# Where attention hands over to the mLSTM stage: batch 0's queries, the gates' second half and ten units

## The reference, cut to what matters

```
x = x + attn(layernorm(x))               # causal softmax, 16 heads of 16; its output is reshaped (heads, time) before W_out
x = x + mlstm(q=layernorm(x), k=v=ctx)   # 8 heads of 32
x = x + moe(layernorm(x))                # 8 experts, top 2, 256 -> 1024 -> 256, exact gelu
# inside mlstm:
pre = 15 * tanh((concat(q, k, v) @ ifgate_w.T + b) / 15); i_pre, f_pre = first 8, last 8
lf  = cumsum(log_sigmoid(f_pre))
log_d[t, s] = lf[t] - lf[s] + i_pre[s] for s <= t;  m[t] = max_s log_d[t, s]
s_mat = (q @ k.T / sqrt(32)) * exp(log_d - m)
h = s_mat @ v / (max(|sum_s s_mat|, exp(-m)) + 5e-5);  h = h * rsqrt(mean(h*h) + 1e-6) * gain
```

## Time and profile before

| | |
|---|---|
| median of 3 runs | 1012.65 us (1009.31 to 1014.28) |
| the profiled execution | 1014.33 us, of which span 1012.5 us |
| PE / PEld busy | 88% / 66% of the span |
| DVE, ACT, POOL busy | 61%, 48%, 52% |
| longest shares of the chain that ended last | PE 57%, DVE 12%, ACT 8%, POOL 6%, issue 6%, DMA 6% |

### The profile page before, as it was taken

The page is one execution under the profiler, slowest core; times in us unless marked ns, Lnnn a source line. Parts: engine busy times, 40 slices in busy tenths (PEclk is TensorE's granted clock), DMA queues, the critical chain, the costliest instruction groups (busy, mean ns, idle before and its releaser), DMA issues.

```text
span 1012.5 us, 31650 instructions
## 1 busy us (share of the span) xinstructions
PE 890.3 (88%) x11877; PEld 664.1 (66%) x11966; DVE 621.5 (61%) x1340; ACT 483.9 (48%) x808; POOL 524.8 (52%) x660
## 2 busy tenths in 40 slices
PE   4798898989896567999899798899999999999995
PEld 3566666666664345666666487687877878787783
DVE  4766777687764345777777756655555555555552
ACT  3556666666765345564655434233333333333331
POOL 2545655655664233568788766643435343444342
PEclk8999999999997878998988879999999999999998
DMA  9112333234233444445555323343333333333222
GB/s 282 52 34 64 82 108 107 75 85 135 76 85 116 105 128 151 128 145 171 168 173 172 102 69 85 81 92 49 51 48 50 50 50 49 51 50 51 49 29 26
DMA packets 133199, 92.97 MB, mean 92 GB/s; under 512 B 75713, under 2 KB 114113, under 8 KB 132929
## 3 DMA queue, kind: packets, MB, share of 16 engines
q1 hardware_dynamic: 119760, 73.10, 26.2%
q0 software_dynamic: 13296, 17.83, 10.6%
HBM read 54.65 MB, written 37.32 MB: 91 GB/s over the span
## 4 chain that ended last, share of the span: by engine, by line
PE 57%; DVE 12%; ACT 8%; POOL 6%; issue 6%; DMA 6%; SPq 2%; POOLq 0%; DVEq 0%; ACTq 0%
PE pair L946 18%; PE pair L960 9%; PE pair L962 7%; PE pair L661 3%; PE pair L675 3%; PE pair L639 3%; POOL sm L1560 3%; DMA o_scr<-On 2%; PE pair L688 2%; DMA STG<-wup_in 2%; PE pair L817 1%; PE pair L912 1%; DMA out_d<-XB 1%; DVE SD L1140 1%; ACT xn L1313 1%
## 5 line engine op out<-in xcount | busy, mean ns | idle before, releaser
L946 PE MATMUL pair<-XTs,WU 128*128 128x128 bf16 x3408 | 287.3, 221 | 9.9 <-DVE XTs L1281 4.1
L946 PEld LDWEIGHTS pair<-XTs,WU 128*128 x3408 | 241.2, 99 | 77.6 <-issue 14.8
L1597 POOL DMA_INDIRECT out_d<-XB x71 | 115.1, 1621 | 209.3 <-DVE XB L1303 180.3
L1473 ACT ACTIVATE Hf<-pair 128x512 f32<-128x512 f32 x142 | 84.8, 597 | 227.8 <-PE pair L946 224.8
L960 PE MATMUL pair<-WD,Hh 128*128 x479 | 181.8, 380 | 0.0
L1294 DVE CAST Hh<-Hf 128x512 bf16<-128x512 f32 x142 | 63.9, 450 | 172.6 <-ACT Hf L1473 172.6
L962 PE MATMUL pair<-WD,Hl 128*128 x568 | 155.1, 273 | 5.0 <-issue 0.2
L1518 POOL TENSOR_SCALAR_AFFINE_SELECT PT<-PT 128x512 f32<-128x512 f32 (+1 forms) x96 | 74.4, 788 | 67.2 <-ACT PT L1332 60.7
L1296 DVE TENSOR_TENSOR Hl<-Hf,Hh 128x512 bf16<-128x512 f32 x142 | 99.8, 703 | 4.9
L1032 DVE TENSOR_REDUCE mxn<-pair 128x4 f32<-128x1024 f32 x64 | 75.3, 1218 | 27.4 <-PE pair L620 27.3
L1140 DVE TENSOR_TENSOR SD<-pair,SD 128x1024 f32<-128x1024 f32 x48 | 58.7, 1223 | 41.0 <-ACT SD L1415 25.5
(11 more groups left out here) (237 smaller groups left out, 1810.8 us busy)
## 6 DMA issues: line engine op xcount, KB each, us to landing
XB<-xs_scr SPq DMA_DIRECT2D x71, 130.0 KB, 2.1
STG<-wup_in SPq DMA_DIRECT2D x32, 256.0 KB, 4.8
q_scr<-SPL SPq DMA_DIRECT2D x16, 512.0 KB, 3.8
STG<-wdn_in SPq DMA_DIRECT2D x32, 256.0 KB, 2.7
o_scr<-On SPq DMA_DIRECT2D x32, 128.0 KB, 4.1
Mm<-o_scr SPq DMA_DIRECT2D x16, 256.0 KB, 3.0
CnT<-ctxt_in SPq DMA_DIRECT2D x16, 256.0 KB, 4.3
CX<-ctx_in SPq DMA_DIRECT2D x16, 256.0 KB, 3.4
```

What stands on the lines that cost most here:

```text
L946: t = e.matmul(upb(j, k)[:, 128 * (fm % 4):128 * (fm % 4) + 128], WU[:, bass.ds(reg[j] * 4096 + off, 128)], XTs[:, r, hx, dk, :], start=n ...
L1473: e.activation(Hf[:, r, hs], upb(j, k), ACT.Gelu).then_inc(gel.sem, 1)
L1597: e.indirect_dma_start(out=out, out_offset=bass.IndirectOffsetOnAxis(ap=XS[:, i % NX, 256:257].bitcast(I32), axis=0), in_=Yf[:, i % NY, :] ...
```

## The change

- `attn_steps`: batch 0's `queries` take the place of Gs and GE at iteration 16 behind PV 14; Gs of q = 0 goes to the end of iteration 15, ahead of AX; GE goes behind the last iteration, ahead of PV 15; MG 17 (the gate sums of batch 12) is added behind PV 15; `contexts` are steps of their own, for batch 0 behind A4 15 and for batch 1 at the end.
- In MG, the maxima's transposes come ahead of the gate sums.
- ScalarE copies the input gates, times 15, from PSUM into `gg_` before Exp; VectorE adds the running sum to it there; the bank is free once Exp has read it. For q = 0 the splitting uses a free part of Q for its remainder, and no longer waits for GE's transposes.
- `rest` spreads over ten units (0,0) to (4,2) other than before: some units take more, GA 13 to 15, XQ 14 and 15 and the gates come later, and A6c 14 sooner.
- The query tiles are set to zero one by one, the first in iteration 15; the order of tiles in SBUF changes so that this part of WD lies over tiles free by then.

```diff
@@ attn_steps
         if i == B:
-            yield "Gs", 0, 0
-            yield "GE", 0, 0
+            yield "queries", 0, 0
             yield "Gp", 0, 0
             yield "Go", 0, 0
             yield "decays", 0, 0
...
         if ok(i - 2):
             yield "A4", i - 2, 0
+        if i == B - 1:
+            yield "Gs", 0, 0
         if ok(i + 2) or ok(i - 4):
             yield "AX", i, 0
...
-    yield "queries", 0, 0
+    yield "GE", 0, 0
     yield "PV", B - 1, 0
+    yield "MG", B + 1, 0
     yield "A4", B - 1, 0
+    yield "contexts", 0, 0
     yield "decays", 1, 0
     yield "queries", 1, 0
+    yield "contexts", 1, 0
@@ mlstm_steps
-    rest = {(0, 0): (("GA", z - 3), ("A6s", z - 2), ("Mm", z), ("X1", z - 1), ("A6n", z - 2), ("A6c", z - 2)),
-            (0, 1): (("A6s", z - 1), ("XQ", z - 2), ("A6n", z - 1)),
-            (0, 2): (("A6c", z - 1), ("X1", z), ("A6s", z), ("GA", z - 2)),
-            (1, 0): (("XQ", z - 1), ("A6n", z)), (1, 1): (("A6c", z), ("GA", z - 1)), (1, 2): (("XQ", z),),
-            (2, 0): (("GA", z), ("Gt", 1)), (2, 1): (("GT", 1),), (2, 2): (("Gs", 1),),
-            (3, 0): (("GE", 1),), (3, 1): (("Gp", 1),), (3, 2): (("Go", 1),)}
+    rest = {(0, 0): (("A6s", z - 2), ("Mm", z), ("X1", z - 1), ("A6n", z - 2), ("A6c", z - 2)),
+            (0, 1): (("A6s", z - 1), ("XQ", z - 2), ("A6n", z - 1), ("A6c", z - 1)), (0, 2): (("X1", z), ("A6s", z)),
+            (1, 0): (("GA", z - 2), ("A6n", z)), (1, 1): (("XQ", z - 1), ("A6c", z)), (2, 0): (("XQ", z),), (2, 1): (("GA", z - 1),),
+            (3, 0): (("GA", z), ("Gt", 1)), (3, 1): (("GT", 1),), (3, 2): (("Gs", 1),), (4, 0): (("GE", 1),), (4, 1): (("Gp", 1),),
+            (4, 2): (("Go", 1),)}
@@ release of the pair (and of tb) by GT
-                w.wait_ge(g_dve.sem, g_dve.at("gg", b))
+                w.wait_ge(g_act.sem, g_act.at("exp", b))
@@ tensor_attn, MG: the gate sums of b - 5 now behind the transposes of Mp
@@ vector_gate_scans
-            e.scalar_tensor_tensor(gg_[:, :], ps[0:64, 0:256], 15.0, cs_, ALU.mult, ALU.add).then_inc(g_dve.sem, 1)
+            e.tensor_tensor(gg_[:, :], gg_[:, :], cs_, ALU.add).then_inc(g_dve.sem, 1)
@@ vector_gate_parts
-            w.wait_ge(g_pe.sem, g_pe.at("emT", q))
+            if q:
+                w.wait_ge(g_pe.sem, g_pe.at("emT", q))
+            rest = (gf, r1b[q])
@@ scalar_gates, GT
+                e.activation(gg_[:, :], ps[0:64, 0:256], ACT.Copy, scale=15.0)
                 e.activation(gf, ps[0:64, 256:512], ACT.Exp, scale=-15.0).then_inc(g_act.sem, 1)
@@ gpsimd_attn, GT
                     w.wait_ge(vmm.sem, vmm.at(B - 1))
+                    e.memset(QS[0][:, 0:2048].bitcast(F32), 0.0).then_inc(qb_z, 1)
...
-            for q in QS:
-                e.memset(q[:, 0:2048].bitcast(F32), 0.0).then_inc(qb_z, 1)
+            e.memset(Q1[:, 0:2048].bitcast(F32), 0.0).then_inc(qb_z, 1)
@@ tensor_mlstm S, and queries
-                    w.wait_ge(qb_z, 2)
+                    w.wait_ge(qb_z, min(b, 1) + 1)
@@ contexts
-            w.wait_ge(vmm.sem, vmm.at(B - 1))
+            w.wait_ge(t2m.sem, t2m.at(B - 1, 1))
```

More of the change, by code:

```diff
@@ L295, in build @@
         ca = ExitStack()
+        WQh = sb("WQh", [128, 2, 768], BF, ca)
+        WQl = sb("WQl", [128, 2, 768], BF, ca)
+        K = sb("K", [128, NQ, 2, 2, 256], F32, ca)
+        Q = sb("Q", [128, NQ, 2, 256], F32, ca)
+        Mp = sb("Mp", [128, 2, 2, 4, 32], BF, ca)
+        MT = sb("MT", [128, 2, 256], BF, ca)
         xTh = sb("xTh", [128, 2, 2, 256], BF, ca)
         xTl = sb("xTl", [128, 2, 2, 256], BF, ca)
-        WQh = sb("WQh", [128, 2, 768], BF, ca)
-        WQl = sb("WQl", [128, 2, 768], BF, ca)
         xn = sb("xn", [128, 2, 256], F32, ca)
-        K = sb("K", [128, NQ, 2, 2, 256], F32, ca)
-        Q = sb("Q", [128, NQ, 2, 256], F32, ca)
         sel = sb("sel", [128, 2, 128], BF, ca)
         mxn = sb("mxn", [128, 2, 2, 4, 2], F32, ca)
-        Mp = sb("Mp", [128, 2, 2, 4, 32], BF, ca)
-        MT = sb("MT", [128, 2, 256], BF, ca)
         OTs = sb("OTs", [128, 4, 256], F32, ca)
@@ L318, in build @@
         gf, cs_ = r1[:, 0, :], r1[:, 1, :]
+        r1b = (Q[0:64, (B - 3) % NQ, 0, :], cs_)
         gg_ = sb("gg_", [64, 256], F32, ca)
@@ L351, in build @@
         te8 = sb("te8", [128, 67, E], F32)[:, 0:NF, :]
-        spare = sb("spare", [128, 172], F32)
+        spare = sb("spare", [128, 168], F32)
         WD = sb("WD", [128, E * 4096], BF)
@@ L487, in high @@
             return t.bitcast(BF).rearrange("p (c h) -> p c h", h=2)[:, :, 1]
-        g_dve = sig("g_dve", [(k, q) for q in range(2) for k in ("cs", "gg", "MM", "run", "neg", "em", "pp")])
+        g_dve = sig("g_dve", [(k, q) for q in range(2) for k in ("cs", "gg", "MM", "run", "neg", *(("em", "pp") if q else ("pp", "em")))])
         g_act = sig("g_act", [(k, q) for q in range(2) for k in ("tanh", "exp", "ln", "em")])
@@ L735, in tensor_attn @@
                         t.then_inc(mpT.sem, 1)
+                    if ok(b - 5):
+                        tensor_gate_sums(e, w, b - 5, ps[:, 1, 0:32])
                 elif kind == "GT":
@@ L1077, in vector_attn @@
                 elif kind == "Gs":
-                    vector_gate_scans(e, w, b, pair_of("GT", b)[:, 0, :])
+                    vector_gate_scans(e, w, b)
                 elif kind == "GE":
@@ L1109, in vector_gate_parts @@
             w.wait_ge(g_dve.sem, g_dve.at("neg", q))
-            w.wait_ge(g_pe.sem, g_pe.at("emT", q))
+            if q:
+                w.wait_ge(g_pe.sem, g_pe.at("emT", q))
+            rest = (gf, r1b[q])
             for n in range(3):
                 for k, src in enumerate((gg_, MM)):
-                    v = src[:, :] if n == 0 else r1[:, k, :]
+                    v = src[:, :] if n == 0 else rest[k]
                     t = e.tensor_copy(pp[:, 3 * k + n, :], v)
@@ L1117, in vector_gate_parts @@
                 for k, src in enumerate((gg_, MM)):
-                    v = src[:, :] if n == 0 else r1[:, k, :]
+                    v = src[:, :] if n == 0 else rest[k]
                     if n < 2:
-                        e.tensor_tensor(r1[:, k, :], v, pp[:, 3 * k + n, :], ALU.subtract).then_inc(dvc.sem, dvc.up())
+                        e.tensor_tensor(rest[k], v, pp[:, 3 * k + n, :], ALU.subtract).then_inc(dvc.sem, dvc.up())
                 w.wait_ge(dvc.sem, dvc.n)
@@ L1153, in vector_mlstm @@
                 elif kind == "Gs":
-                    vector_gate_scans(e, w, b, tb)
+                    vector_gate_scans(e, w, b)
                 elif kind == "GE":
@@ L1671, in sync_attn @@
                     queries(e, w, b)
+                elif kind == "contexts":
                     contexts(e, w, b)
```

4 lines of the change are left out of this document (1 added, 3 removed).

## The result

Medians: 1008.45 us after the change (12 runs, 1005.76 to 1010.12), 1012.65 before (12 runs, 1009.31 to 1017.57); ratio 0.9949, 95% interval 0.9933 to 0.9965. By the ratio the change gains 5.1 us of the 12 forecast (by the medians 4.2), and its time lies 7.8 above the predicted 1000.7, at the upper end of the range of 994.5 to 1009. The profiled execution took 1006.74 us around a span of 1005.0.

What follows compares the result with a forecast made beforehand. The bound taken was the matmul engine's waits between attention's last batch and the second stage's first unit. First S 12.5 us sooner, +0.5 over ten units: 12 off 1012.65 gives 1000.7 us, range 994.5 to 1009.

Steps and rivals of the forecast that it cites:

- Step 1: ScalarE's copy of the gates, taken at 0.38 us, frees the bank so that T0 of batch 15 starts 1.8 us sooner.
- Step 2: Scans before batch 11's low half: query split ends at 323.9; no cost if it ties with T0 15, 0.5 us if late.
- Step 3: GE behind attention's T2: T0's other half 3.5 us sooner, batch 12's norm 5.9 us sooner, PV 15 at 336.1.
- Step 4: Batch 0's queries issued by 327.6 and landed by 331.1, so the 6.92 us wait ahead of the first S goes.
- The carry: From batch 5 on the order is as before, so the experts start 12 us sooner.
- the rest over ten units: New order of left-over work, batches 0 to 4: sum +1 us, bounds -5 and +8, taken as +0.5.
- The first rival: ScalarE's waits in batches 0 to 4 do not overlap: +6 in place of +0.5, 1006.2 us; chance 0.17.
- gate sums 13: They held batch 1's D unit 3.98 us for batch 15's residual; moved behind D and S: -3, bounds -4 and 0.
- The norm: Batch 15's norm, ahead of batch 14's transposes, holds ScalarE from D's exponential of unit (1,1): +2.5 us, bounds 0 and 4.
- The gates: Table loads and scans move to batch 3, gg's 2.21 us wait goes: -2; GE and splitting in batch 4: +2.
- The clock: Matmul engine longer at 1.2 GHz in the 16 batches: up to 5 us per 10 us, 1019.2 with 37; chance 0.06.
- Another transfer in the queries' place: Decays or batch 14's merged output come late, first units wait, 6.9 us of gain go: 1007.5 us; chance 0.09.

Runs made afterwards that it cites:

- copy_only: Kernel before plus only ScalarE's copy of the gates, its release and VectorE's plain add: 1020.18 us, ratio 0.9991.
- again: The changed kernel run once more, unedited, beside its variants: 1006.74 us, ratio 0.9942 to the kernel before.
- old_rest: Changed kernel with the `rest` table of the kernel before: 1000.05 us, ratio 0.9872; run once more, 0.9847.
- groups 2 to 4: Follow-up kernels in three sets, each on one chip beside the kernel before, whose medians there were 1022.91, 1019.97 and 1020.34 us.
- group 1: First set of follow-up kernels, run on one chip beside the kernel before, whose median there was 1012.66 us.
- norm_order: Changed kernel with query transposes XQ 14 put ahead of the norm of batch 15 again, in unit (1,0): 1006.36 us, ratio 0.9925.
- ge_bank: Changed kernel with the second half's GE transposes in a free part of bank 7, not waiting for hh: 1015.84 us, ratio 0.9941.
- context_first: old_rest with batch 14's context moved ahead of unit (0,2), as in the changed kernel: 1011.13 us, ratio 0.9908.
- old_rest2: old_rest once more, unedited, as the base of the last group: 1006.94 us, ratio 0.9847.
- queries_late_old_rest: old_rest with batch 0's queries issued behind GE, near their old place: 1015.28 us, ratio 0.9937.

## Why the prediction was wrong, step by step

**Right: the way to the first S.**
- Step 1: T0 15 starts 4.3 us sooner, 2.7 after the 1.65 from ahead of the hole; 1.8 forecast. copy_only, which isolates the step, has 1.9. The copy costs 0.27 from its start to Exp's (314.96 to 315.23), not 0.38: the two overlap. By the budget of the Trainium skill ("ScalarE: Activation LUTs", "Rules for kernel authors"), about 0.3 us and 0.83 ns an element, it would be an estimated 0.51 us; but that budget is for an ACTIVATE whose bias is a pointer operand, and this copy has a constant scale. The trace has less, 0.37 us busy.
- Step 2: the last scan step ends at 320.83 and the query split behind it at 321.42, PV 14 starts at 321.48: the tie that I had forecast, at no cost.
- Step 3: T0's other half at 325.60, 327.25 with the 1.65 (327.8 forecast); PV 15 at 333.39, 335.0 (336.1). It ran in 2.81 us, not 4.44, in a stage granted 0.87 in place of 0.79. "Again" had a grant of 0.81, 4.49 us for PV 15 and still the same first S, 341.30: there the wait for o_scr was only 0.86, so the shorter PV 15 was worth nothing. With GE in its old place the first S came 4.6 us later (another chip; 5.1 counted from the gates' transposes): the step is real.
- Step 4: queries issued up to 326.6, 328.2 with the 1.65 (327.6 forecast), decays up to 333.5 by issue. The first S did not wait for a transfer of its own, but 2.54 us for the tile behind o_scr's write. That wait, not in my list, ate what PV 15 had gained: 12.6 us against 12.5. The step's price, 6.9, is 4 to 7 by experiment.
- The carry: what is ahead at batch 5 stays ahead to the end. Batches 5 to 14 take 128.7 before, 129.8 and 129.9 after, 129.4 in old_rest. In groups 2 to 4 they take 131.5 to 141.3, and there this is not tested, since the kernel before was not profiled.

**Wrong: "the rest over ten units", +0.5 taken.** It measured +7.5 (81.84 - 74.34), and +6.3 in "again", at the upper end of its bounds (+8). The first rival, "the spread rest takes back half", gave +6 and 1006.2, and its size is what came. Its reason, waits for ScalarE's exponentials ahead of D, is 4.0 of the 7.8 us between "again" and old_rest by the matmul engine's waits, and the wait ahead of GE, at the end of the gates' chain, is another 4.0. Since the change with the table of before is at 1000.05, the whole miss lies in this term. Its parts, by batch spans in us (old_rest is that of group 1):

| term | as predicted | before | changed kernel, again | measured against before | old_rest |
|---|---|---|---|---|---|
| gate sums 13, context 14 (batch 0) | -3 + 1.5 | 17.17 | 17.76, 17.93 | +0.6, +0.8 | 17.05 |
| norm 15 ahead of XQ 14 (batch 1) | +2.5 | 12.41 | 15.38, 15.25 | +3.0, +2.8 | 12.16 |
| gates a batch later (batches 2 to 4) | -2 + 2 | 44.76 | 48.70, 47.46 | +3.9, +2.7 | 43.59 |

So the norm was about right, and two lines failed: the credit of 3 for gate sums 13, and the zero for the gates. The first is off by 2.1 to 2.3 us and the second by 2.7 to 3.9, of the 5.8 to 7.0 that the whole sum is off.

- *Gate sums 13.* The credit of 3 was for the 3.98 for which they had held D up while the residual was late. That stall is the end of a chain over o_scr's write of batch 15, its merged read, the residual's transposes and VectorE's add. The chain did not move as far as the first S: the merged read is issued 6.3 us behind the first S in the kernel before (362.14), and 10.2 behind it in the changed kernel (351.75). In old_rest, which keeps the gate sums ahead of D, the stall is still there, 3.17 + 0.79 us, only that most of it now stands ahead of the residual's transposes:

```profile
355.51 1.09 PE L894 MATMUL pair<-CF,Mm 128*128 128x128 f32 x4 [3.17 <-DMA Mm<-o_scr]
...
357.38 0.81 PE L770 MATMUL pair<-WGs,SPL 128*128 128x16 bf16 x24 [0.79 <-DVE XB L1153]
```

  In the changed kernel the same transposes wait 1.81:

```profile
354.91 0.96 PE L893 MATMUL pair<-CF,Mm 128*128 128x128 f32 x4 [1.81 <-DMA Mm<-o_scr]
```

  Moving the gate sums could not remove that. Then D waits 2.21 us (358.08) for an exponential that stands behind the context's transfer, 2.08; this was in the sum, as +1.5 for a wait of 1 to 2 us.
- *The norm.* Against the kernel before, +2.5 was forecast and +2.8 to +3.0 came. ScalarE stood 5.1 to 5.8 us, and behind the late exponential come VectorE's product of D, PV and the next D. The price depends on what else has moved: from old_rest the order alone costs +6.2 in batch 1 and +4.7 by medians, and in the changed kernel to undo it (norm_order) gives back 1.0 in batch 1.
- *The gates.* I summed -2 and +2. The wait of 2.21 us for gg did go, and old_rest's batches 2 to 4 are 1.2 us shorter than before; copy_only shows no gain clear of its noise. The +2 for GE and the splitting a batch later was too small: against old_rest the same batches take 3.9 to 5.1 us more. GE stands behind a chain over several engines: scans, the sums of the output's norm, GpSimd's root of them (2.9 us), hh. In "again", one batch later, the scans stand behind a product of D for which VectorE waits 6.32 us:

```profile
402.51 1.23 DVE L1146 TENSOR_TENSOR SD<-pair,SD 128x1024 f32<-128x1024 f32 x1 [6.32 <-ACT SD L1422]
...
406.44 0.28 DVE L1105 TENSOR_SCALAR MM<-MM 64x256 f32<-64x256 f32 x1
...
407.71 2.91 POOL L1567 TENSOR_TENSOR sm<-sm,mhalf 128x16 f32<-128x16 f32 x1 [3.48 <-DVE sm L1175]
```

  The last of the scans' steps starts 2.5 us after the batch's first S (406.44, 403.98), in old_rest with it (388.44, 388.50), and GE waits 5.61 in place of 1.55. Whether that wait is the whole price is open: ge_bank has 1.89 in its place and batch 4 is 2.6 us shorter, but its ratio is the same, and the runs can't tell 2.6 us. Moved alone, the gates cost +3.5 by medians, but in those kernels batches 2 to 4 are not longer (45.08 and 44.07, against 43.59 and 45.69 in old_rest's two executions).

**The rivals.** The clock: 0.79 in the stretch of 81.84 us, but 0.85 in "again" at 80.64; at nearly the same grant (0.84) old_rest takes 72.80, so the clock is not the cause. Another transfer in the queries' place: this happened in small. The first S waits 2.54 us behind o_scr's write, and still comes 12.6 us sooner; and the matmul engine waits 2.2 to 2.4 us for o_scr's merged reads ahead of the residuals, for which the kernel before does not wait. By these waits that is where the credit for gate sums 13 went; no run moves that read alone. That the change does not do what it says is excluded by that too.

**My own test fired.** I had written "wrong if batch 5 starts less than 8 us earlier though the first S came 12 sooner": it started 6.8 earlier, 423.42 against 430.21.

**Still open**: how the gates' place costs its 3.5 to 5 us, since it falls in batches 2 to 4 in the changed kernel and behind batch 4 where the gates are moved alone; what would be left of the norm's price in the changed kernel with all else put back; and the size of the context's share, since context_first had its base on other chips only. Not tried: the new table on the kernel before. There the bank's next user in unit (3, 1) would wait for gg, which VectorE writes a unit later; the copy is what allows this order, so copy and table can't be judged apart in that direction.

The best version is old_rest: the change, with the table of before. It beats the kernel before on two chips, 0.9872 and 0.9847, and the changed kernel on the one on which both ran.

## What to carry to other kernels

When an instruction that waits is moved on an engine that works in order, price it by what stands behind it on that engine, and by who waits for that. The length of its own wait is not the price: here 5.1 to 5.8 us of waiting cost about 3 us in one kernel, and 4.2 us of waiting cost 4.7 or more in another. Before you credit a wait that goes away, follow the chain that ended it, and ask whether that chain moves as far as the work around it: the 3.98 us ahead of the gate sums came back, nearly to the digit, ahead of the residual's transposes, because the read they wait for had moved 10.4 us where the first S had moved 14.3. And where a change has a part that opens a hole's end and a part that rearranges what follows, time them apart: here one part brought 12.6 us and the other took 6.7 back.

## What the runs showed of the hardware

- Two ACTIVATEs of 64x256 from PSUM, one behind the other, are 0.37 us each by the profile and 0.27 apart. The first costs less than its busy time where the second follows.
- The first DMA of batch 0's queries took 2.33 us to issue at 322.40 (L1702), but 0.72 in "again" and 1.78 in old_rest2 at the same place, and 0.99 at its later place in queries_late_old_rest. What it waited for the profile does not show.
- The kernel before took 1012.66 on one chip and 1022.91 on another: 1.0%, twice the change's own effect.
